# A graph network on one core: the ranks of the low edges move from the fill to the first place

## What is computed

```python
def _sage_conv(x, src, dst, Wl, Wr, b):
    n = x.shape[0]
    agg = jax.ops.segment_sum(x[src], dst, num_segments=n)
    deg = jax.ops.segment_sum(jnp.ones_like(dst, dtype=x.dtype), dst, num_segments=n)
    mean = agg / jnp.maximum(deg, 1.0)[:, None]
    return mean @ Wl + x @ Wr + b
h = jnp.maximum(_layernorm(x, axis=-1), 0.0)
h = jax.nn.relu(_sage_conv(h, src, dst, Wl1, Wr1, b1))
h = jax.nn.relu(_sage_conv(h, src, dst, Wl2, Wr2, b2))
h = jax.nn.relu(_sage_conv(h, src, dst, Wl3, Wr3, b3))
out = x + _sage_conv(h, src, dst, Wl4, Wr4, b4)
```

## Time and profile before

| | us |
|---|---|
| median of three runs | 659.34 |
| lowest and highest run | 659.32, 663.9 |
| span of the profiled execution | 659.6 |

### The profile page before, as it was taken

How to read it: one execution, slowest core, us unless ns; L and a number is a source line. 1 busy time by engine, 2 the same in 40 slices (tenths; PEclk the granted TensorE clock), 3 DMA queues, 4 the chain that set the end, 5 groups by cost and what they waited for, 6 DMA issues and landing times.

```text
span 659.6 us, 10093 instructions
## 1 busy us (share of the span) xinstructions
PE 622.7 (94%) x4071; PEld 345.0 (52%) x4072; DVE 276.2 (42%) x526; ACT 179.1 (27%) x381; POOL 42.8 (6%) x91
## 2 busy tenths in 40 slices
PE   5679998899999899998999999899999999999998
PEld 4436555555554455553444444444445555646686
DVE  6978877678788779711212121111120100101011
ACT  3886854265643623210111011121110000000000
POOL 8002300000000000000000000000001011010110
PEclk9977999999999999999999999999999999999999
DMA  8301200510231122242534431445430223032030
GB/s 265 95 0 49 79 1 2 183 51 6 69 33 52 34 52 65 50 136 48 160 87 117 122 85 45 101 111 144 120 121 1 54 70 112 0 112 83 30 113 33
DMA packets 63526, 50.98 MB, mean 77 GB/s; under 512 B 35510, under 2 KB 48347, under 8 KB 63480
## 3 DMA queue, kind: packets, MB, share of 16 engines
q1 hardware_dynamic: 63124, 49.74, 26.6%
q0 software_dynamic: 240, 0.37, 0.2%
q10 hardware_dynamic: 116, 0.24, 0.1%
HBM read 28.15 MB, written 16.60 MB: 68 GB/s over the span
## 4 chain that ended last, share of the span: by engine, by line
PE 78%; DMA 7%; DVE 7%; ACT 3%; issue 2%; SPq 1%; POOL 1%; DVEq 0%; ACTq 0%; POOLq 0%
PE agg_ps L2241 27%; PE window_ps L2241 18%; PE lin_ps L2159 6%; PE lin_ps L2176 5%; PE window_ps L2072 4%; PE lin_ps L2135 3%; DMA rdeg_d<-newH 3%; PE lin_ps L2029 2%; PE window_ps L2217 2%; PE agg_ps L2217 2%; DMA rdeg_d<-rdeg 2%; DVE early L1445 1%; PE lin_ps L2263 1%; ACT counts L1794 1%; PE lin_ps L2184 1%
## 5 line engine op out<-in xcount | busy, mean ns | idle before, releaser
L2241 PE MATMUL agg_ps<-counts,H 128*128 128x512 f16 (+3 forms) x1026 | 235.0, 355 | 1.6 <-DVE aggT L1536 1.5
L2241 PEld LDWEIGHTS agg_ps<-counts,H 128*128 128x128 f16 (+1 forms) x1026 | 79.2, 98 | 56.6 <-issue 10.8
L1794 ACT ACTIVATE counts<-window_ps 128x400 f16<-128x400 f32 x150 | 73.6, 507 | 64.5 <-PE window_ps L2072 50.6
L1438 DVE TENSOR_TENSOR counts<-early 128x2048 f16<-128x2048 bf16 x66 | 77.9, 1215 | 6.3 <-PE window_ps L2072 4.8
L2241 PE MATMUL window_ps<-counts,early 128*128 128x512 f16 (+2 forms) x346 | 77.6, 379 | 0.0
L2241 PEld LDWEIGHTS window_ps<-counts,early 128*128 128x128 f16 (+1 forms) x346 | 33.7, 98 | 41.5 <-issue 3.4
L2241 PE MATMUL window_ps<-counts,H 128*128 128x512 f16 (+2 forms) x291 | 55.3, 346 | 0.0
L1536 DVE SCALAR_TENSOR_TENSOR aggT<-agg_ps,columns,rdeg 128x512 f32<-128x512 f32 (+1 forms) x27 | 16.9, 659 | 81.2 <-PE agg_ps L2241 62.6
L2072 PEld LDWEIGHTS window_ps<-counts 128*128 128x128 f16 x412 | 30.8, 99 | 34.3 <-issue 4.6
L1438 DVE TENSOR_TENSOR early<-early 128x1024 f16<-128x1024 bf16 (+1 forms) x69 | 43.8, 684 | 7.4 <-PE window_ps L2072 5.9
L2241 PE MATMUL agg_ps<-counts,early 128*128 (+4 forms) x297 | 46.5, 314 | 0.0
(11 more groups left out here) (241 smaller groups left out, 631.9 us busy)
## 6 DMA issues: line engine op xcount, KB each, us to landing
selfT<-hT_d SPq DMA_DIRECT2D x18, 512.0 KB, 4.2
hT_d<-newT SPq DMA_DIRECT2D x12, 512.0 KB, 4.5
rdeg<-rdeg_d SPq DMA_DIRECT2D x22, 256.0 KB, 4.1
counts<-in_x_dram SPq DMA_DIRECT2D x6, 512.0 KB, 7.9
hT_d<-counts SPq DMA_DIRECT2D x6, 512.0 KB, 3.4
newH<-in_x_dram SPq DMA_DIRECT2D x6, 512.0 KB
out_dram<-newT SPq DMA_DIRECT2D x5, 512.0 KB
hT_d<-newT SPq DMA_DIRECT2D x6, 256.0 KB, 3.9
```

The lines of the kernel that those rows point to most:

```text
L1438: v.tensor_tensor(hots_of(group).rearrange("p r a (n d) -> p r a n d", d=2), pairs.unsqueeze(1).unsqueeze(1).broadcast_to([P, n, 2, P // 2 ...
L1794: a.activation(counts[:, :, 2 * w * WIN:2 * (w + 1) * WIN].rearrange("p t (a w) -> p a t w", a=2), window_bank(FILL_AT[w])[:, 0:2 * KEYS]. ...
L2241: last = m((agg_ps, window_ps)[bank][:, h, 0:n], tile[:, part, h * P:(h + 1) * P], counts[0:rows_, k, chunk_cols(c, n)], start=first and p ...
```

## The change

Calls change their place in the dicts; nothing is added to or taken from what is computed. The four `below` and `rank_low`, with `first_rows(3)`, go from the fill to the first place, and `bases_late`, `turn_bases`, `late_rows`, `select_late`, `late_sources`, `spread_sources`, `late_tables` and the norms go later in it. `early_tables(0)` comes ahead of `h0_moments(0)`, which goes behind pair 2; the roots, relus and shifts of the first chunks go to later pairs. ACT's moments of chunks 4 and 5 go from the fill to the first place and later in it. SP's and GpSimd's lists keep their order. In the changed listing the lines stand one to four lower.

```diff
@@ DVE: ahead of the fill @@
             choose_early(1, chosen_next, NEXT_EVEN)
-            h0_moments(0)
             early_tables(0)
@@ DVE: fill, then first place @@
-            between = {0: lambda: h0_moments(1), 2: lambda: h0_shift(0),
-                       9: lambda: (h0_moments(2), early_tables(1)), 10: lambda: h0_shift(1),
-                       12: lambda: (below(0), h0_low_part(0)), 17: lambda: h0_low_part(1), 18: lambda: h0_shift(2),
-                       19: lambda: edge_tables(), 25: lambda: below(1), 28: lambda: (below(2), below(3)),
-                       30: lambda: plan_high()}
+            between = {2: lambda: h0_moments(0), 5: lambda: h0_shift(0), 7: lambda: h0_moments(1),
+                       9: lambda: early_tables(1), 10: lambda: h0_shift(1), 13: lambda: h0_low_part(0),
+                       16: lambda: h0_moments(2), 17: lambda: h0_low_part(1), 18: lambda: h0_shift(2),
+                       20: lambda: edge_tables(), 30: lambda: plan_high()}
...
-            first_round = {0: lambda: (h0_moments(3), bases_late(2)), 1: lambda: (degrees(0), h0_low_part(2)),
-                           3: lambda: bases_late(3), 5: lambda: (late_rows(), h0_shift(3)), 7: lambda: h0_shift(4),
-                           9: lambda: h0_low_part(3), 10: lambda: square_weights(), 11: lambda: late_tables(2),
-                           12: lambda: h0_low_part(4), 13: lambda: h0_shift(5), 15: lambda: h0_low_part(5),
-                           16: lambda: (late_tables(3), h0_shift(6)), 21: lambda: h0_low_part(6)}
+            first_round = {0: lambda: (h0_moments(3), below(0)), 1: lambda: (degrees(0), h0_low_part(2), below(1)),
+                           2: lambda: (below(2), below(3)), 5: lambda: (h0_shift(3), bases_late(2)),
+                           6: lambda: bases_late(3), 7: lambda: h0_shift(4), 8: lambda: late_rows(),
+                           9: lambda: h0_low_part(3), 12: lambda: h0_low_part(4), 13: lambda: (h0_shift(5), square_weights()),
+                           14: lambda: late_tables(2), 15: lambda: h0_low_part(5), 16: lambda: h0_shift(6),
+                           19: lambda: late_tables(3), 21: lambda: h0_low_part(6)}
@@ ACT: fill, then first place @@
-            h0_root(0)
-            between = {0: lambda: (h0_relu(0, (0, 1)), h0_relu(0, (2, 3)), h0_high_part(0)),
-                       6: lambda: (h0_root(1), h0_root(2)), 9: lambda: (h0_relu(1, (0,)), h0_high_part(1)),
-                       11: lambda: h0_copy(0), 13: lambda: whole_sources(2, TUSED, whole[1]),
-                       17: lambda: (h0_relu(2, (0, 1)), h0_relu(2, (2, 3))), 18: lambda: own_copy(0),
-                       21: lambda: h0_moment(4, 0), 24: lambda: h0_moment(4, 1),
-                       25: lambda: (h0_copy(1), h0_moment(4, 2)),
-                       26: lambda: (h0_moment(4, 3), h0_high_part(2), own_copy(1)),
-                       31: lambda: (first_rows(3, slice(0, MID), degree_ps[:, 0:MID]), h0_moment(5, 0), h0_moment(5, 1))}
+            between = {2: lambda: h0_root(0), 4: lambda: (h0_relu(0, (0, 1)), h0_relu(0, (2, 3)), h0_high_part(0)),
+                       8: lambda: h0_root(1), 9: lambda: (h0_relu(1, (0,)), h0_high_part(1)),
+                       12: lambda: h0_copy(0), 14: lambda: whole_sources(2, TUSED, whole[1]), 17: lambda: h0_root(2),
+                       19: lambda: (h0_relu(2, (0, 1)), h0_relu(2, (2, 3))), 20: lambda: own_copy(0),
+                       25: lambda: (h0_copy(1), h0_high_part(2)), 27: lambda: own_copy(1)}
...
-            first_round = {0: lambda: h0_root(3), 1: lambda: h0_moment(5, 2),
-                           3: lambda: (h0_root(4), h0_moment(5, 3)), 5: lambda: h0_copy(2),
-                           6: lambda: h0_high_part(3), 7: lambda: (h0_moment(6, 0), h0_moment(6, 1), own_copy(2)),
-                           8: lambda: (h0_high_part(4), h0_copy(3)), 9: lambda: late_sources(2),
-                           10: lambda: h0_moment(6, 2), 11: lambda: (spread_sources(2), h0_root(5), own_copy(3)),
-                           12: lambda: h0_moment(6, 3), 13: lambda: (h0_high_part(5), h0_root(6)),
-                           14: lambda: late_sources(3), 15: lambda: h0_copy(4), 16: lambda: own_copy(4),
-                           17: lambda: (norms(0), h0_high_part(6)), 18: lambda: norms(1),
-                           20: lambda: spread_sources(3), 21: lambda: norms(2), 24: lambda: copy_degrees(0)}
+            first_round = {0: lambda: (h0_root(3), h0_moment(4, 0), h0_moment(4, 1)),
+                           2: lambda: (h0_moment(4, 2), h0_moment(4, 3)), 3: lambda: h0_root(4),
+                           4: lambda: first_rows(3, slice(0, MID), degree_ps[:, 0:MID]), 5: lambda: h0_copy(2),
+                           6: lambda: (h0_high_part(3), h0_moment(5, 0)), 7: lambda: (h0_moment(5, 1), own_copy(2)),
+                           8: lambda: (h0_high_part(4), h0_copy(3)), 9: lambda: (h0_moment(5, 2), h0_moment(5, 3)),
+                           10: lambda: (h0_root(5), h0_moment(6, 0)), 11: lambda: (own_copy(3), h0_moment(6, 1)),
+                           12: lambda: (h0_moment(6, 2), h0_moment(6, 3), h0_root(6)), 13: lambda: late_sources(2),
+                           14: lambda: h0_high_part(5), 15: lambda: (spread_sources(2), h0_copy(4)),
+                           16: lambda: own_copy(4), 17: lambda: (late_sources(3), h0_high_part(6)),
+                           20: lambda: norms(0), 21: lambda: spread_sources(3), 22: lambda: norms(1),
+                           24: lambda: (norms(2), copy_degrees(0))}
@@ PE: fill, then first place @@
-                       27: lambda: h0_turn(1), 28: lambda: (rank_low(), own_products(1))}
-            first_round = {3: lambda: turn_bases(), 4: lambda: h0_turn(2), 7: lambda: own_products(2),
-                           8: lambda: (h0_turn(3), select_late(2)), 11: lambda: own_products(3),
-                           13: lambda: select_late(3), 15: lambda: h0_turn(4), 16: lambda: own_products(4),
-                           17: lambda: squares(0), 19: lambda: squares(1), 21: lambda: squares(2),
-                           24: lambda: turn_degrees(0)}
+                       26: lambda: h0_turn(1), 28: lambda: own_products(1)}
+            first_round = {3: lambda: rank_low(), 4: lambda: h0_turn(2), 7: lambda: (turn_bases(), own_products(2)),
+                           8: lambda: h0_turn(3), 11: lambda: own_products(3), 12: lambda: select_late(2),
+                           15: lambda: h0_turn(4), 16: lambda: (own_products(4), select_late(3)),
+                           20: lambda: squares(0), 21: lambda: squares(1), 23: lambda: squares(2), 24: lambda: turn_degrees(0)}
```

## The result

The changed kernel takes 674.72 us (median of 4 runs, 671.31 to 677.3) against 659.33 (4 runs, 658.93 to 663.9). The ratio of the comparison is 1.0181 with a 95% interval of 1.0135 to 1.0228: slower by 1.8%. The forecast was slower by 7.7 us; the ratio makes it 11.9 (671.3), the two medians 15.4, the two profiled spans 15.9 (659.6 and 675.5). The profiled run of the changed kernel took 677.3, 1.8 more than its span, and was the slowest of the four.

A forecast was written before the change was run, and what follows sets the result against it. DVE was taken to bound the fill, and TensorE, without gaps, most of the first place. From 659.6, -3.7 for the fill and +3.6, +1.2, +0.4, +1.6, +2.05, +2.1, +0.5 gave 667.35, less 0.3: 667.0 us, range 656 to 672.

The forecast's parts named there:

- fill, T' - T: Fill's end, where `add_degrees` begins (T before, T' after): 46.3 against 50.03, -3.7 us.
- the low ranks' chain: First place, `rank_low`, `first_rows(3)`, then `bases_late` on DVE: idle DVE time carried to TensorE, +0.4 us, bounds 0 and 2.
- ACT behind `own_copy(2)`: First place: chunk 5's last two moments stand ahead of a pair copy TensorE wants, +1.6 us.
- ACT behind `own_copy(3)`: First place: moments and a root on ACT delay a copy that TensorE wants 3.6 us on, +2.05 us.
- sum at E: All terms up to the second chunk's `add_degrees`, which ends the first place: +7.75 us.
- Rival (a): First place: TensorE's clock stays low longer and reaches `rank_low`, 3.5 us more, 670.5 us; chance 0.10.
- the low stretch behind T': Start of first place: the earlier 6.8 us at the lower clock stays, with the clock up when `rank_low` comes.
- four waits of 5.05: Fill: DVE waits on the table load (1.0), two later roots (1.55, 1.0) and three hot groups (1.5).
- the ring: Fill: three hot groups on DVE, held up when chunk 2's relus delay copies and so TensorE, about 1.5 us.
- Rival (c): Fill falls to DVE's own work, ending at 41 to 42, -8.8 us; 658 to 662 us; chance 0.25.
- Rival (b): First place: waits on DVE and ACT reach TensorE by half, 7.85 us become 3.9; 663 us; chance 0.18.
- Rival (d): Short fill (-8.8), ACT waits hidden, low clock after the fill gone (-3.4); 651.0 us; chance 0.07.

The follow-up runs named there:

- e5: The changed kernel with its first place kept, but the fill in the earlier order, without `below` and without ACT's moments; ratio to before 1.0148.
- e12: The kernel before with spare 128x128 matmuls where TensorE waits in the fill, ahead of pairs 21 to 25 and behind the last pair; ratio to before 0.9938.
- e4: The changed kernel with extra matmuls repeating work (select of piece 2, turn of chunk 4) where TensorE waits in the first place; ratio to before 1.0149.
- e1: The changed kernel with ACT's moments of chunks 4 to 6 back where they stood before; ratio to before 1.0124.
- e9: The changed kernel with ACT's list alone reordered from k = 9 on: chunk 5's and 6's moments later, `late_sources(2)` ahead of chunk 6's; ratio to before 1.0216.
- e3: Ranks moved to the first place as in the changed kernel, with the earlier fill order and ACT's moments where they were before; ratio to before 1.0082.
- e10: The changed kernel with the moments and roots of chunks 0 to 2 earlier in its fill; ratio to before 1.0171.
- e8: The fill of e5 with another first place: ACT's moments spread, `rank_low` at k = 4, ACT's and DVE's queues reordered; ratio to before 1.0101.

## Why the prediction was right, and where it failed

| term | forecast | measured |
|---|---|---|
| fill, T' - T | -3.7 | -2.6 |
| `rank_low` | +3.6 | +3.5 |
| `below` ahead of the thin group | +1.2 | +1.2 (0.45 of wait, 0.75 at the lower clock) |
| the low ranks' chain | +0.4 | +1.15 (0.46 + 0.69) |
| ACT behind `own_copy(2)` | +1.6 | +1.52 |
| ACT behind `own_copy(3)` | +2.05 | +1.8 (0.34 + 1.71, less 0.25 of before) |
| `late_tables(2)` | +2.1 | +2.05 |
| `late_tables(3)` and low part 6 behind it | +0.5 | +2.07 (0.21 + 0.37 + 1.49) |
| the lower clock behind that | 0 | +4.5 |
| sum at E | +7.75 | +15.2 of 16.0 |

The rest is small: a wait costs some 0.15 more than the idle time in its bracket. From the sum at 89.37 to the group of 92.02 is 2.65, where the next group follows its sum by 0.43: a price of 2.2 for the 2.05 shown.

**Right:** the direction, and the mechanism in the first place. The queue of ACT behind each own copy, worked out by durations and two banks, and of DVE's tables behind it, came out within 0.25 us for all three terms; e5 repeats the same waits behind another fill. The group behind `below` came at T' + 9.9, forecast T' + 10.0. ACT's timeline behind `own_copy(3)`, one moment ahead of the first copy and two and a root ahead of the second:

```profile
83.13 1.08 ACT L1774 ACTIVATE counts<-lin_ps 128x512 f32<-128x512 f32 x2 [2.23 <-PE lin_ps L2026]
...
85.27 0.50 ACT L1793 ACTIVATE counts<-window_ps 128x400 f16<-128x400 f32 x1
...
88.21 0.48 ACT L1793 ACTIVATE counts<-window_ps 128x400 f16<-128x400 f32 x1
88.60 0.46 ACT L1861 ACTIVATE aggT<-degree_ps 128x358 int32<-128x358 f16 x1
```

**Luck:** the range of 656 to 672 holds the 671.3 of the ratio, by 0.7, but not the median of the four runs, 674.72, and in the profiles the loss is twice the forecast. Rival (a)'s 670.5 is nearest to 671.3, but not for its reason: `rank_low` took 3.46 at the upper clock.

**The step that failed** is the treatment of the clock. The sum kept the low stretch behind T' and took the clock as up from there, a term of nothing; rival (a) let it fall for longer, but only onto `rank_low`, and gave as its counterargument that the new waits were "shorter than the idle before 50.03". That idle was 1.98; the longest new wait was 2.05, the others 1.71 and less, and the clock fell all the same, at 91 and again at 108, at a price of some 4.5 us. A sure number was not to be had, since the same waits cost 3 us less in e5, but nothing was too little. The rule of the Trainium skill that stood beside that rival (TensorE: Matmul & The Clock Gate, "Why this matters for your kernels"), that idle time lowers the clock and steady work brings it back, agrees with e12, where spare work in the waits kept it at 1.00, and e4 fits it; that the clock stayed up behind 1.91 us of idle in e1 and 2.73 in e9 shows that here such a wait alone didn't decide.

**Sizes off.** `late_tables(3)`: the sum saw its groups late and took one place of room, but not that low part 6 stands behind it in DVE's list and that TensorE's sums of the last source tiles wait for it (1.49). The low ranks' chain: TensorE waited for it in two places, 1.15 in all, where 0.4 was carried. The fill: 1.1 us less gain than forecast, about what T' varies by. The 1.7 of the early tables is no term of its sum; the new order was in it as four waits of 5.05, and by runs the order costs 3.3 to 3.6 (e1 and e3, the changed kernel and e5). Taking the moments out of ACT's fill has no term in it, and 3.0 to 3.3 of the gain hang on that (e1, e3). Of the four waits, the table load was to cost 1.0 and cost nothing; the roots cost 2.25 and 1.01 for 1.55 and 1.0, but without them T' moves by 0.85 (e10); the ring cost 1.0 for 1.5. And the step from span to time took the profiled span for a time: a run takes 1.8 us more than its span.

Rival (c) fell: T' was 47.5, not 41 to 42, and even the best fill here, without ranks, moments and with the old order, ended at 43.4 (e8). Rival (b) fell: the ACT waits reached TensorE whole. Rival (d) fell by both, and its 3.4 for the low stretch behind T was 2.2 by e12.

**Open:** why the tables-first order makes the fill 3 to 5 us longer; e10 speaks against the roots, and ACT's relus near the end were only argued. What decides whether the clock falls behind a wait. Whether an order of the first place exists that holds this work. The span behind E differed by up to 4.7 us between profiles of kernels that have the same work there; that was not followed up.

## What to carry to other kernels

Work moved from a stretch that another engine bounds to one where the busiest engine has no gap costs its full length there, and each short wait that comes with it may, not must, be paid again in that engine's clock; so count the idle pieces, not only their sum. A wait in a hand-written queue can be forecast to a few tenths from the durations of what stands between two signals, but each thing that stands behind the late one in its list must be asked who waits for it. Where TensorE must wait, a little spare work into a free bank can be cheaper than the wait.

## What the runs showed of the hardware

TensorE's clock fell behind waits of 1.5 to 2.05 us in most runs (the changed kernel, e3, e5, e10), and not in all: it stayed at 1.00 behind 1.91 in e1, where e3 fell behind 1.90 in the same first place, and behind 2.73 in e9. It stayed up when TensorE did throwaway matmuls in such places (e4: 1.00 for 0.50 from 91 to 97.6; e12: 1.00 for 0.51 from 37.9 to 44.7 and 51.3 to 58.1). The 100 small matmuls of `add_degrees` took 3.56 us at the lower clock and 3.22 at the upper, while 16 of 128x512 took 5.71, mostly at the lower, and 3.63. A comparison of 98x512 in f16 took GpSimd 1.82 us against DVE's 0.344, and DVE's one-hot groups took 17 to 18% longer on the mean beside it (461 to 545 ns, 350 to 411). A table load of 1.28 us was followed by ACT's next instruction at once.
